# Attention value products issued in two halves of four matmuls instead of one burst of eight

## The reference

```python
x = x + recurrence(layernorm(x))          # minGRU-like scan over the sequence, 192 inner channels
x = x + ffn(layernorm(x))

def ffn(x):                               # H = 16 heads of 8 channels, E = 8 experts, top 2
    h = layernorm(x, ln1)
    q, k, v = (h @ W).reshape(B, 256, 16, 8) for W in (Wq, Wk, Wv)
    scores = einsum("bqhd,bkhd->bhqk", q, k) / sqrt(8)
    attn = softmax(scores)                # fp32, over 256 keys
    ctx = einsum("bhqk,bkhd->bqhd", attn, v).reshape(B, 256, 128)
    x = x + ctx @ Wo
    m = layernorm(x, ln2)
    ...                                   # softmax gate, two experts of 512 hidden units, weighted sum
    return x + moe_out
```

## The kernel before, in words

| place | what follows the scores |
|---|---|
| 2, 6, 10, 14 | `pv` of the group that ended 3 steps before |
| 3 | `b1_shift` in blocks 2 to 9; `logits` (router, 4 fp32 matmuls, 8 records) in blocks b with (b - 7) % 4 = 0 or 1 |
| 5 | `ctx_t`: four 128x128 transposes (L1517) of the block before |
| 7 | `max_t`: two matmuls that transpose the next block's maxima |
| 9 | `ctx_n`: two transposes (L1524) |
| 12 | `ctx_o`: output projection, two fp32 matmuls |
| 13 | `tp5_group`: four transposes (L1341) in blocks b with (b - 6) % 4 = 0 or 1 |

## Time and profile before

### The profile page before, as it was taken

One profiled execution on the slowest core, in us unless ns is written; L12 is line 12 of the kernel. 1 busy time (PEld: TensorE's weight loads), 2 busy tenths in 40 slices (PEclk: granted clock), 3 DMA queues, 4 the chain that ended last, 5 costly groups with the idle time before them and its releaser, 6 DMA issues.

```text
span 1079.4 us, 25392 instructions
## 1 busy us (share of the span) xinstructions
PE 792.2 (73%) x8366; PEld 489.8 (45%) x8367; DVE 813.8 (75%) x1600; ACT 589.7 (55%) x1198; POOL 529.8 (49%) x669
## 2 busy tenths in 40 slices
PE   3587566588888988888888888861999999995000
PEld 2355444223444434443334334441788888885000
DVE  7788689577886788888887878527888888888522
ACT  6754278436766677777546667740655555552000
POOL 9500099401225461615017486845677336665775
PEclk9999889868988899999768999975999999999555
DMA  7820023401111111211001221001455445543432
GB/s 183 314 84 1 1 79 117 161 26 46 46 50 38 43 47 51 61 31 32 16 26 44 59 58 56 22 20 32 112 137 132 114 107 130 134 125 97 131 82 71
DMA packets 132071, 84.16 MB, mean 78 GB/s; under 512 B 54520, under 2 KB 117628, under 8 KB 131982
## 3 DMA queue, kind: packets, MB, share of 16 engines
q1 hardware_dynamic: 123790, 66.20, 21.2%
q0 software_dynamic: 8192, 16.79, 5.8%
HBM read 30.25 MB, written 41.94 MB: 67 GB/s over the span
## 4 chain that ended last, share of the span: by engine, by line
PE 57%; DVE 19%; POOL 9%; issue 6%; ACT 3%; DMA 1%; SPq 0%; POOLq 0%; ACTq 0%; DVEq 0%
PE bank L1337 54%; DVE arena L1100 11%; POOL HT L757 3%; POOL Z L757 3%; DVE arena L1036 2%; POOL xh L501 1%; PE bank L1341 1%; POOL rr L497 1%; PE bank L1517 1%; PE bank L1524 1%; DVE Z L1020 1%; DVE mom L955 1%; DVE Z L1027 1%; ACT Z L806 1%; ACT arena L836 0%
## 5 line engine op out<-in xcount | busy, mean ns | idle before, releaser
L1100 DVE TENSOR_REDUCE arena<-bank 128x2 f32<-128x512 f32 x512 | 339.3, 688 | 97.0 <-PE bank L1337 94.9
L855 ACT ACTIVATE arena<-bank 128x512 f32<-128x512 f32 x512 | 292.8, 596 | 155.0 <-PE bank L1337 153.0
L1337 PE MATMUL bank<-QK 32*128 32x256 f16 (+1 forms) x2048 | 193.9, 291 | 79.0 <-DVE arena L1100 66.5
L1337 PE MATMUL bank<-w2p,QK 128*128 x1280 | 216.5, 246 | 1.4 <-DVE arena L1300 1.4
L928 ACT ACTIVATE arena<-bank,b1s 128x256 f32<-128x256 f32 x320 | 125.3, 475 | 102.7 <-PE bank L1337 99.0
L1337 PE MATMUL bank<-arena,w1h 128*128 128x256 f16 x640 | 165.3, 275 | 12.3 <-DMA arena<-expert_in 9.4
L689 POOL DMA_INDIRECT expert_in<-HT,idx x128 | 133.3, 1041 | 83.5 <-PE bank L1337 47.0
L1337 PEld LDWEIGHTS bank<-QK 32*128 32x128 f16 (+1 forms) x2048 | 59.8, 94 | 215.5 <-ACT arena L855 163.0
L1337 PE MATMUL bank<-arena,VA 128*32 128x256 f32 x2048 | 150.4, 415 | 0.7 <-ACT arena L855 0.7
L1337 PEld LDWEIGHTS bank<-w2p,QK 128*128 128x128 f16 x1280 | 124.0, 98 | 10.8 <-issue 1.7
L1295 DVE TENSOR_TENSOR QK<-arena,QK 128x1024 f16<-128x1024 f32 x80 | 98.0, 1225 | 2.7
(11 more groups left out here) (158 smaller groups left out, 1152.7 us busy)
## 6 DMA issues: line engine op xcount, KB each, us to landing
QK<-qk_parts SPq DMA_DIRECT2D x96, 128.0 KB, 2.6
expert_in<-arena SPq DMA_DIRECT2D x40, 256.0 KB, 3.1
expert_out<-arena SPq DMA_DIRECT2D x80, 128.0 KB
qk_parts<-arena SPq DMA_DIRECT2D x16, 512.0 KB, 2.8
X<-x SPq DMA_DIRECT2D x8, 512.0 KB, 5.7
wst<-w SPq DMA_DIRECT2D x16, 256.0 KB, 2.8
out<-arena SPq DMA_DIRECT2D x16, 256.0 KB, 2.6
expert_in<-HT,idx POOLq DMA_INDIRECT x128
```

The costliest lines, as they stand in the source:

```text
L855: nc.scalar.activation(PT[t % 8], bank[2 + t % 2][:, :], ACT.Exp, scale=DH ** -0.5)\
L1100: V.tensor_reduce(nmax[n % 2][:, :, 4 * j + g], bank[u % 2][:, :].rearrange("p (q t) -> p q t", q=2), AX.X, ALU.max, negate=True).then_inc ...
L1337: return nc.tensor.matmul(dst, lhsT, rhs, start=start, stop=stop)
```

## The change

`pv` gets a second argument, the half of the keys. A group's four matmuls of half 0 are issued behind the scores of step 4G + 5, those of half 1 behind the scores of step 4G + 7; before, all eight stood behind step 4G + 6. By place, the halves stand at 1, 3, 5, 7, 9, 11, 13 and 15. `pv_done` is signalled by the second half. The waits for the value tile and the context bank are made before half 0 of a block's first group. Number, shape, type and operands of the matmuls are the same.

```diff
-            def pv(G):
+            def pv(G, kt):
                 b, g = G // 4, G % 4
                 gp, gg = g // 2, g % 2
                 pe.wait_ge(exp_done, 4 * G + 4)
-                if g == 0:
+                if g == 0 and kt == 0:
                     pe.wait_ge(va_ready, 2 * b + 2)
                     if b >= 2:
                         pe.wait_ge(ct_ready, b - 1)
-                for kt in range(2):
-                    for j in range(4):
-                        c = 64 * (8 * kt + 4 * gp + j) + 32 * gg
-                        last = mm(bank[4 + b % 2][32 * j:32 * j + 32, SL * gp:SL * gp + SL],
-                                  VA[b % 2][:, 8 * kt + 4 * gp + j, 32 * gg:32 * gg + 32],
-                                  PT[(4 * G + j) % 8][:, SL * kt:SL * kt + SL],
-                                  start=gg == 0 and kt == 0, stop=gg == 1 and kt == 1)
-                last.then_inc(pv_done, 1)
+                for j in range(4):
+                    last = mm(bank[4 + b % 2][32 * j:32 * j + 32, SL * gp:SL * gp + SL],
+                              VA[b % 2][:, 8 * kt + 4 * gp + j, 32 * gg:32 * gg + 32],
+                              PT[(4 * G + j) % 8][:, SL * kt:SL * kt + SL],
+                              start=gg == 0 and kt == 0, stop=gg == 1 and kt == 1)
+                if kt == 1:
+                    last.then_inc(pv_done, 1)
...
-                if c % 4 == 2 and 6 <= t < 16 * NB + 6:
-                    pv((t - 6) // 4)
+                if c % 2 == 1 and 5 <= t < 16 * NB + 5:
+                    pv((t - 5) // 4, (t - 5) % 4 // 2)
```

## The result

The changed kernel took 1082.59 us in the median of its 20 executions, the kernel before 1096.65 us in 20 of its own. The ratio is 0.9919 with a 95% interval of 0.989 to 0.9948; it counts fast executions alone and leaves out as slow those more than 1.5% above the shortest of the same kernel, which for the kernel before are all above about 1098 us, while the two medians with every execution in them stand at 0.987. The prediction had 1105 us against 1097, so the time lies in the range but moved the other way. One execution of the changed kernel lasted 3226 us; nothing here explains it.

A forecast was written before the change was run, and what follows sets the result against it. In the attention TensorE and VectorE wait for one another, neither being the bound alone. Steps +6.7 us and clock +3 us, taken as 10 on a median of 1097, gave 1107, set to 1105 us; range 1073 to 1135.

The forecast's parts named there:

- The five rules: Attention at full clock: timings of steps, maxima, exponentials, value products and extras (logits, transposes, copies), trusted to about 0.1 us a block.
- The half at 0.57: Value product in the attention: each half holds TensorE 0.57 us, two 1.14 where one product held it 1.01.
- The step behind a half at 0.89: Attention groups without extras: scores and half take 0.32 + 0.57 = 0.89 us before the next step.
- The collisions: Places 3, 5, 7, 9, 13: half and extra behind one step hold the next back 1.29 to 1.88 us, beyond VectorE's 1.28.
- the plain group: Group without extras, places 14 to 2 of the next block: 3.22 us before, 2.80 after, 0.42 less.
- the sum, +6.7 us: Whole attention: four blocks +1.43 us, five such fours in blocks 10 to 29 +7.1; with first and last blocks +6.7.
- 0.1 less: Bound on the sum: if switching from half to extra costs 0.1 us less than from scores to extra, -2.5 us.
- the clock, +3 us: Attention's granted clock, mean 0.91 in the profile: +3 us charged for the new order, bounds -20 and +25.
- Every switch on the path: Slower rival: second half's 0.13 us and scores' drain 0.11 paid in all 128 groups, 31 us, 1128 us; chance 0.16.
- VectorE is fed evenly: Faster rival: extras hide as before, each of 128 groups saves 0.42, 54 us, 1043 us; half gives 1070; chance 0.12.
- The sign set for it: Sign that the forecast is wrong: the attention's clock moves by more than 0.04.
- The clock rival: Slower rival: five more attention blocks fall to half clock, 5 x 3.3 + 6.7 = 23 us, 1120 us; chance 0.12.

The follow-up runs named there:

- the first series: Runs in which all kernels took about 5% longer; both kernels repeated without edit: kernel before 1151.31 us, changed kernel 1131.94 us, ratio 0.9819.

## Why the prediction was wrong

**What held.** The five rules, and most of the gaps that they gave: 13 of the 16 in the logits block to 0.03 us or better. The half at 0.57. The step behind a half at 0.89 (0.90 in the trace). The collisions: taken away, a block without logits falls from 13.79 to 13.10, forecast 13.2. In the block shown TensorE waits for VectorE and once for ScalarE, so there the waits of GpSimd and SP cost nothing, as forecast. And the plain group (places 14 to 2) gains 0.42, as forecast: 3.22 before, and from 458.70 to step 2 of block 16 2.8 us.

**The step that failed first: the sum, +6.7 us.** It measured -2 to -6 at an equal clock. Four blocks at full clock went from 55.59 to 55.97, +0.4, not +1.4. Two terms were mis-sized. The 0.78 copy ahead of exponential 1 overlaps it (copy from 446.39 to 447.16, exponential from 447.05), so step 3 starts 0.2 earlier. And `max_t` behind a half starts after 0.46 (451.80 to 452.26), where the transposes start after 0.57 (449.92 to 450.49): its weights are 16 columns wide, the half's 32, against 128. I had put "0.1 less" for such a switch among the bounds but gave it to none of the extras. With 0.4 in place of 1.4 for each of five fours, the sum is 6.7 - 5.3 = +1.4. The first blocks gained more than the 0.9 forecast: block 1 went from 13.47 to 13.02, blocks 2 to 4 from 13.87 to 13.62, block 5 from 14.33 to 14.16, 1.4 together, and block 0 some 1.3 on its own. In the last two, 0.8 instead of 0.4. That brings the sum to about -1; the other few us up to -6 are not assigned; blocks that run partly at half clock, for which I had no rules, may hold them. (The terms of the recorded sum add up to 6.8, not 6.7.)

**The step that failed second, and the larger: the clock, +3 us.** It measured about -7 on the usual times and -15 in the first series. I read one execution's mean clock of 0.91 as a property of the kernel and charged the change against it. That execution was shorter than all 20. The old order's executions vary from 1081 to 1111 us with the clock; the new order's hardly vary, 1078 to 1086. The median lies 15.4 us above the profiled execution in the one case and 3.6 in the other. In the prediction that distance was carried over unchanged, and here was the gain. That the known times spread from 1081 to 1097, with one of 1225, should have made the clock a rival on both sides. It stood there as a price for slower, and on the other side only as a remark. The sign set for it, the attention's clock moving by more than 0.04, could not show it either: the two profiles have 0.91 and 0.90, since a profile is one execution.

**The rivals.** "Every switch on the path" falls: TensorE still waits 42.3 us for the maxima. A price of the switch is there: 0.11 us lie between the two cases above. The Trainium skill (TensorEngine Tiling (Array Packing), Key Properties) says that a change of tiling mode drains TensorE, and the trace agrees with that as far as these 0.11 us go. "VectorE is fed evenly" was right in the direction but not in the mechanism: VectorE's wait fell from 88.5 to 82.9 us, 5.6 and not 54. The clock rival had the right mechanism with the wrong sign.

**What is open.** What exactly makes the granted clock fall was not settled. In the kernel before it fell behind a stretch like this one at the head of block 16:

```profile
464.90:468.40 3.50, 2.91 (x36) 1.69 (x36) 2.81 (x5) 3.00 (x7) 0.96 (x3) 1.00 0.42 112
468.40:471.80 3.40, 3.40 (x30) 1.68 (x33) 2.37 (x6) 2.00 (x4) 1.28 (x2) 0.51 0.02 5
```

A matmul ran for 2.91 of 3.50 us, and eight of its 36 records were the logits, which stream 8 columns each. With filler at places 0 and 2 next to them the clock stayed full in block 16. That the logits are the cause and not merely near it was not tried: no run here took them away. They can't be the whole of it. Block 2 of the kernel before has none, and its clock falls at 260, while `b1_shift` runs (the first line below; 1.05 us in the blocks where the clock stays full). Block 29 of the changed kernel has neither, and its clock falls at 673.7 (the second line; a half at full clock is 0.64):

```profile
259.47 1.15 PE L1337 MATMUL bank<-aff,wst 128*128 128x1 f32 x8
...
673.72 1.06 PE L1337 MATMUL bank<-arena,VA 128*32 128x256 f32 x8
```

## What to carry to other kernels

When the executions of a kernel spread more than 1% and the granted clock spreads with them, the profile of one of them is no base for a sum: work out time at half clock for each, and price a new order once for steps at full clock and once for the clock. Splitting a long piece of TensorE work brought 0.4 us here where the halves stood alone behind their steps, and lost more than that where they shared a step with other work (at full clock four blocks got 0.4 longer in sum); write down what follows each step before moving one. And a denser order can lose by the clock what it won in steps; a few matmuls in a wait that exists anyway are a cheap test of that.

## What the runs showed of the hardware that I had not expected

- Matmuls that nobody needs made the kernel faster: 256 of them in the kernel before, ratio 0.9945 (0.9909 to 0.9981), 384 in another series 0.9876 (0.9825 to 0.9928), with the clock up from 0.839 to 0.855 and from 0.864 to 0.888.
- An even flow in which a matmul runs 634 of 649 us went with 1.2 GHz for most of the attention (0.56), once the clock had fallen. The Trainium skill (TensorE: Matmul & The Clock Gate, What's actually happening) says that the clock is set by how busy TensorE has been; here a matmul stands in the records for all 19.70 us of block 17, and the clock stayed at 0.50.
- One us more at half clock cost 0.25 to 0.36 us, not 0.5, over executions of the same kernel: while TensorE is slow, its waits shrink (in block 16 above it is busy 2.91 of 3.50 us at full clock, 3.40 of 3.40 at half).
- The two halves of a value product hold TensorE 1.14 us at full clock, for 1.01 in one piece. A half held it 0.57 us where weights of 128 columns came next and 0.46 where `max_t` with its 16 columns did.
